# Summing eight experts' weighted outputs: from products and a separate tree of sums to multiply-adds in place

## The reference, cut to what matters

```python
E, D, H = 8, 64, 256                      # experts, channels, hidden
h = gelu(einsum('end,edh->enh', xe, W1) + b1[:, None, :])
y = einsum('enh,ehd->end', h, W2) + b2[:, None, :]      # [expert, token, channel]
sel = take_along_axis(transpose(y, (1, 0, 2)), top_idx[:, :, None], axis=1)
out = (weights[:, :, None] * sel).sum(axis=1)           # two best experts of each token
x = t + out                                             # t: the residual, x2 in the kernel
```

## Time and profile before

| What | Value |
|---|---|
| Runs | 319.32, 317.60, 319.03 us, median 319.03 |
| The profiled execution, its own time | 318.64 us |
| Its span, first to last instruction | 316.9 us |
| TensorE busy | 279.8 us (88%) |
| ScalarE busy | 256.5 us (81%) |
| VectorE busy | 242.5 us (77%) |
| GpSimd busy | 119.8 us (38%) |
| Mean granted TensorE clock | 0.981 of full speed |

### The profile page before, as it was taken

The page is one execution under the profiler, slowest core; times in us unless marked ns, Lnnn a source line. Parts: engine busy times, 40 slices in busy tenths (PEclk is TensorE's granted clock), DMA queues, the critical chain, the costliest instruction groups (busy, mean ns, idle before and its releaser), DMA issues.

```text
span 316.9 us, 8774 instructions
## 1 busy us (share of the span) xinstructions
PE 279.8 (88%) x3434; PEld 191.4 (60%) x3434; DVE 242.5 (77%) x720; ACT 256.5 (81%) x490; POOL 119.8 (38%) x124
## 2 busy tenths in 40 slices
PE   7976998868799898799899999799879999988894
PEld 2552566645467575476577665576667787766462
DVE  6999769799958999659588997586956453589474
ACT  2587678899897999997988899988949898877562
POOL 5040042405142604054466240090836644279130
PEclk9999799989999999999999999999979999999998
DMA  7910000000000000000000000000000000000000
GB/s 157 289 34 0 2 3 4 2 0 0 2 2 4 3 2 2 0 2 8 3 11 2 2 2 0 3 3 8 2 10 2 1 2 2 10 1 11 2 0 17
DMA packets 7190, 4.86 MB, mean 15 GB/s; under 512 B 5089, under 2 KB 6830, under 8 KB 7086
## 3 DMA queue, kind: packets, MB, share of 16 engines
q1 hardware_dynamic: 7150, 4.31, 5.4%
HBM read 2.04 MB, written 0.52 MB: 8 GB/s over the span
## 4 chain that ended last, share of the span: by engine, by line
PE 38%; DVE 27%; ACT 15%; POOL 11%; issue 8%; DMA 1%; SPq 0%; DVEq 0%; ACTq 0%; POOLq 0%
DVE prod L833 4%; PE m_ps L1583 4%; ACT wk L1256 4%; PE zl_ps L1472 4%; PE zh_ps L1469 3%; ACT wk L1251 3%; PE ga_ps L1503 3%; PE ga_ps L1505 3%; PE ga_ps L1504 3%; POOL lx L531 3%; POOL prod L522 3%; PE m_ps L1564 2%; PE m_ps L1566 2%; DVE samp L848 2%; PE m_ps L1447 1%
## 5 line engine op out<-in xcount | busy, mean ns | idle before, releaser
L833 DVE TENSOR_TENSOR prod<-ga_ps,wx 128x480 f32<-128x480 f32 x96 | 61.8, 650 | 36.0 <-PE ga_ps L1505 35.8
L522 POOL TENSOR_TENSOR prod<-prod 128x960 f32<-128x960 f32 (+1 forms) x20 | 39.4, 1969 | 128.2 <-DVE prod L833 128.2
L1503 PE MATMUL ga_ps<-v_all,wk 128*128 128x80 f16 x576 | 80.5, 204 | 6.2 <-DVE prod L833 5.8
L1251 ACT ACTIVATE wk<-zh_ps 128x512 f16<-128x512 f32 x108 | 65.2, 603 | 20.6 <-PE zh_ps L1469 19.5
L1505 PE MATMUL ga_ps<-v_all,wk 128*128 128x80 f16 x576 | 80.5, 204 | 0.0
L1504 PE MATMUL ga_ps<-v_all,wk 128*128 128x80 f16 x576 | 80.5, 204 | 0.0
L1503 PEld LDWEIGHTS ga_ps<-v_all,wk 128*128 128x128 f16 x576 | 57.5, 100 | 18.4 <-issue 9.5
L1256 ACT ACTIVATE wk<-zl_ps 128x512 f16<-128x512 f32 x108 | 65.0, 602 | 0.0
L1504 PEld LDWEIGHTS ga_ps<-v_all,wk 128*128 128x128 f16 x576 | 57.9, 101 | 6.9 <-issue 0.6
L1505 PEld LDWEIGHTS ga_ps<-v_all,wk 128*128 128x128 f16 x576 | 58.1, 101 | 0.0
L1469 PE MATMUL zh_ps<-tab,sel_hi 128*128 128x512 f16 x108 | 42.4, 393 | 6.8 <-ACT wk L1251 5.5
(11 more groups left out here) (278 smaller groups left out, 592.4 us busy)
## 6 DMA issues: line engine op xcount, KB each, us to landing
v_all<-still SPq DMA_DIRECT2D x1, 1440.0 KB, 9.8
h_all<-in_W SPq DMA_DIRECT2D x1, 512.0 KB
w_s<-in_W SPq DMA_DIRECT2D x1, 512.0 KB
x_tok<-in_x SPq DMA_DIRECT2D x1, 384.0 KB, 4.1
out_dram<-x_tok SPq DMA_DIRECT2D x6, 64.0 KB, 1.6
w_high<-w_high SPq DMA_DIRECT2D x1, 256.0 KB, 2.9
const<-in_table SPq DMA_DIRECT2D x1, 218.0 KB, 2.5
vec<-in_vectors SPq DMA_DIRECT2D x1, 132.5 KB
```

What stands on the lines that cost most here:

```text
L522: then(pool.tensor_tensor(p[:, 0:3, :], p[:, 0:3, :], p[:, 3:6, :], ALU.add))
L833: dve.tensor_tensor(prod[q % 2][:].rearrange("p k n -> p (k n)")[:, f * PB * NV:(f + 1) * PB * NV] .rearrange("p (n c l) -> p n c l", n=PB ...
L1251: act.activation(wk[n % WR][:, 0, :], zh_ps[:], ACT.Relu, scale=W_SCALE).then_inc(s_wkh, 1)
L1503: pe.matmul(to, w_h, high, start=True, stop=False)
```

## The change

Each of the six calls of `outputs_in` now issues 16 instructions in place of two: for each expert e and each of the two tiles, `out_s = m_ps * wexp[e] + (x2 or out_s)`, on 64 columns. The weight is a pointer scalar (one number per partition). The two tiles take turns, and each instruction waits through `s_chain` for the one of its own tile before it. `combine` and its places in the tables are gone, and so are `yb`'s use there and `s_y_rd`. VectorE posts `s_out` at the end of the string, and `expert_out` waits for that in place of `s_y_rd`.

```diff
-            def combine(d, i):
-
-                pool.wait_ge(s_y_rd, 2 * d + i + 1)
-                then(pool.tensor_tensor(yb[:, :, 0:4, :], yb[:, :, 0:4, :], yb[:, :, 4:8, :], ALU.add))
-                then(pool.tensor_tensor(yb[:, :, 0:2, :], yb[:, :, 0:2, :], yb[:, :, 2:4, :], ALU.add))
-                then(pool.tensor_tensor(yb[:, :, 0, :], yb[:, :, 0, :], yb[:, :, 1, :], ALU.add))
-                pool.tensor_tensor(out_s[:, d * TP + 2 * i:d * TP + 2 * i + 2, :], yb[:, :, 0, :], x2[:, 2 * i:2 * i + 2, :],
-                                   ALU.add).then_inc(s_out, 1)
...
-                    for i in range(2):
-                        if has_d and n == at["combine"][i]:
-                            combine(j - 1, i)
...
             def outputs_in(d, i):
 
                 dve.wait_ge(s_yt, 2 * d + i + 1)
-                dve.wait_ge(s_chain, seen["wexp"])
-                if i == 1 or d > 0:
-                    dve.wait_ge(s_out, 2 * d + i)
-                for t in range(2):
-                    ins = dve.tensor_tensor(yb[:, t, :, :], m_ps[2 + t].rearrange("p (e c) -> p e c", c=C),
-                                            wexp[:, 2 * i + t, :].unsqueeze(2).to_broadcast([P, E, C]), ALU.mult)
-                ins.then_inc(s_y_rd, 1)
+                acc = [seen["wexp"]] * 2
+                for e in range(E):
+                    for t in range(2):
+                        at = out_s[:, d * TP + 2 * i + t, :]
+                        dve.wait_ge(s_chain, acc[t])
+                        ins = dve.scalar_tensor_tensor(at, m_ps[2 + t][:, e * C:(e + 1) * C], wexp[:, 2 * i + t, e:e + 1],
+                                                       x2[:, 2 * i + t, :] if e == 0 else at, ALU.mult, ALU.add)
+                        if e < E - 1:
+                            acc[t] = mark(ins)
+                ins.then_inc(s_out, 1)
...
                     if d == LAST:
-                        pe.wait_ge(s_y_rd, 2 * d)
+                        pe.wait_ge(s_out, 2 * d)
                 if 2 * m == E and d < CHUNKS - 1:
-                    pe.wait_ge(s_y_rd, 2 * d + 1)
+                    pe.wait_ge(s_out, 2 * d + 1)
```

More of the change, by code:

```diff
@@ L67 @@
              "second_norm": 0}
-POOL_FIRST = {"tap_tree": [4, 14, 23, 31], "combine": [35.5, 22.5], "conv_rstd": 10, "inner_rstd": 21.5, "input_rstd": 27}
+POOL_FIRST = {"tap_tree": [4, 14, 23, 31], "conv_rstd": 10, "inner_rstd": 21.5, "input_rstd": 27}
 PE_MIDDLE = {"input_t": 0, "convolve": [4, 6.5, 6.5, 7.5], "project": 5, "image_t": [9.5, 12], "conv_t": 13.5,
@@ L81 @@
               "bias_rows": 4.5, "router_parts": 12.5, "w1_low": [8, 9.5, 11, 17], "outputs_in": [23.5, 35]}
-POOL_MIDDLE = {"tap_tree": [16.5, 22.5, 25.5, 34.5], "combine": [27, 35.5], "conv_rstd": 21, "inner_rstd": 14,
+POOL_MIDDLE = {"tap_tree": [16.5, 22.5, 25.5, 34.5], "conv_rstd": 21, "inner_rstd": 14,
                "input_rstd": 34}
@@ L99 @@
             "half_expert_weights": 68.5, "lane_sums": [20, 20.5, 29.5, 46.5, 48, 57, 65]}
-POOL_LAST = {"tap_tree": [4, 19.5, 21.5, 35, 42.5, 53.5, 66.5, 71.5], "combine": [37, 53.5], "conv_rstd": 30.5,
+POOL_LAST = {"tap_tree": [4, 19.5, 21.5, 35, 42.5, 53.5, 66.5, 71.5], "conv_rstd": 30.5,
              "inner_rstd": 2.5, "input_rstd": 47, "half_inner_rstd": 44.5, "router_exp": 17.5, "half_router_exp": 71}
@@ L446, in build @@
         s_ysb = sem("s_ysb")
+        s_out = sem("s_out")
         s_yt = sem("s_yt")
-        s_y_rd = sem("s_y_rd")
-        s_out = sem("s_out")
         s_st_out = sem("s_st_out")
```

## The result

The changed kernel's four runs are 326.06, 326.74, 327.61 and 329.09 us, median 327.18, against 319.0 for the kernel before (four runs, 317.6 to 319.32). The ratio estimated from all the runs is 1.0279, with a 95% interval of 1.0244 to 1.0314: slower by 2.8%. The two medians are 8.2 us apart, which is 2.6%. The forecast was 326.4 in a range of 322 to 332. The profiled execution took 326.06 us, its span 324.3, 7.4 more than before.

A forecast was written before the change was run, and what follows sets the result against it. No engine was taken to have much room, TensorE's in-order queue being nearly full, so stops there are lost almost whole. Six call terms (+7.6 us) on 318.64 us, plus half the 0.4 us median offset, gave 326.4 us, range 322 to 332.

The forecast's parts named there:

- The pace: VectorE's 16 multiply-adds start about 0.20 us apart, so each call holds the queue 3.15 us, 1.95 more than before.
- Rival A: Serial string on VectorE: pace 0.32 us, hold 5.1 us per call, together +19.3, 338 us; chance 0.06.
- rival D: Heavy pointer scalar and PSUM read on VectorE: pace 0.27 us, 6.7 us more, 333 us; chance 0.13.
- The 4.5 us computed for a string without overlap: If VectorE's pipe empties before each next start, a call takes 16 x 0.28 us, sum 15.7 us.
- GpSimd: GpSimd some 18 to 20 us less busy without `combine`; VectorE's three copies near 0.96 us at chunks 0 and 1, pair 0.
- The moved wait: TensorE's `expert_out` waits for all 16 instructions (3.27 us) instead of two products (1.3 us), stalling at three calls.
- The terms: Net losses at the six calls, in order: 0.5, 1.55, 0.85, 1.95, 0.8, 1.95 us, sum +7.6 us.
- (1,1): Call at chunk 1, tile pair 1, on the chain, TensorE already standing 1.3 us: all of it, +1.95 us.
- (2,1): Call at chunk 2, tile pair 1, on the chain, TensorE standing 1.20 us for `weigh`: all of it, +1.95 us.
- Rival B: Absorption: TensorE's waits for ScalarE's `wk` (2.6 us) vanish too, +5.0 us, 323.8 us; chance 0.13.
- Rival C: String no dearer than two products: -1.05 + 3e - 0.35 us, e extra per call; 317.8 us without e; chance 0.04.

The follow-up runs named there:

- one_tile_first: Changed kernel with each call running all eight experts of one tile, then of the other; median 344.65 us, ratio 1.0804.
- scrap_sums: Changed kernel with GpSimd still making the four sums of `combine`, on a scrap tile nothing reads; median 329.14 us, ratio 1.0327.
- vector_tree: Kernel before with the four sums of `combine` moved to VectorE, banks set free behind the two products; median 325.31 us, ratio 1.0216.
- late_release: Kernel before with TensorE's `expert_out` held back until VectorE's cast of the weights, at pair 0 of chunks 0 and 1; median 322.70 us, ratio 1.0107.
- fill_wait: Changed kernel with ten idle multiplications on TensorE in its wait behind the call at (1,1); median 325.35 us, ratio 1.0227.
- defer_call: Changed kernel with the call of (1,1) issued in the next body, behind `weigh` and `lane_sum`; median 324.32 us, ratio 1.0193.
- half_string: Changed kernel with eight multiply-adds per call, experts 4 to 7 left out; median 318.71 us, ratio 0.9994.

## Why the prediction was right, point by point

- **The pace.** 0.197 taken, 0.192 measured, in every call; the hold 3.07 us for 3.15. Rival A's 0.32 belongs to a string in which each waits for the one before (`one_tile_first`: 0.32 inside a tile, 0.304 over the call), rival D's 0.27 doesn't occur: neither the pointer scalar nor the PSUM operand costs anything beyond the row L631. The 4.5 us computed for a string without overlap did not come either.
- **GpSimd.** 18.3 us less busy, in the 18 to 20 expected; the copies at 0.96 us as written. The relief is worth 0.9 to 1.6 us in the profile (`scrap_sums`).
- **The moved wait.** Expected stalls 1.2, 1.2, 0.8; found 1.13, 1.13, 0.74. Setting the banks free early removed them (`vector_tree`), and what they cost is the stall less the waits given back (`late_release`).
- **The terms.** Expected 0.5, 1.55, 0.85, 1.95, 0.8, 1.95, sum 7.6; found 0.3, 1.5, 0.7, 3.0, 0.8, 1.4, sum 7.7. The sum owes its closeness to errors of opposite sign (+1.05 at (1,1), -0.2, -0.05, -0.15 and -0.55 elsewhere), and that part is luck.
- **The mis-sized term is (1,1)**: "All of it, +1.95" is right for the call (1.8 in `fill_wait`), but the clock is missing from it, 1.2 us. TensorE had been standing 1.3 us there before, and its clock had fallen then too, from 233.2 to 236.6 us, but behind the projections and for nothing. With 1.9 more its wait is 3.16 us, and the clock was at half from the projections until 242 us. I had costed a stall as its own length only.
- **(2,1)** is smaller than 1.95 by 0.5. TensorE's wait grew by 2.69 - 1.20 = 1.49 us. Before, the call started 0.46 us behind VectorE's `y_s` (0.30 of that idle), and now 0.08 behind. Before and after:

```profile
279.97 0.16 DVE L919 TENSOR_TENSOR y_s<-y_s,y_r 128x2 f32<-128x2 f32 x1
280.43 1.29 DVE L979 TENSOR_TENSOR yb<-m_ps,wexp 128x512 f32<-128x512 f32 x2 [0.30 <-DVE y_s L919]
...
285.32 0.16 DVE L906 TENSOR_TENSOR y_s<-y_s,y_r 128x2 f32<-128x2 f32 x1
285.40 0.48 DVE L967 SCALAR_TENSOR_TENSOR x_tok<-m_ps,wexp,x 128x64 f32<-128x64 f32 x2
```

 The call holds the queue 1.88 us longer (3.07 - 1.19) and starts 0.38 sooner, which makes the 1.5. What the call stood waiting for in the kernel before isn't shown; I had not looked at what stood ahead of it. TensorE's clock fell behind the wait of 2.69 us as well (0.50 from 290 to 292 us), but `defer_call`, without a fall there, takes the same 1.4 us for the step.
- **Rival B** (absorption) did not come: TensorE's waits for `wk` at L1459 are 5.6 us over the span, 5.5 before. ScalarE stood still with TensorE, as written against it.
- **Rival C** needed a short string. `half_string` is that case, and it came out at no change, within 0.3 us of the formula, though by the other path that is told there: that nearness is luck too.

## What to carry to other kernels

Cost an instruction on an engine with time to spare by its place, not by the engine's share: the same 3.1 us string cost 3.0 us more than before ahead of the sum that TensorE stood waiting for and 0.6 us behind it. When a stall of TensorE is lengthened, look at how long it stands there already, and add what the lower clock costs on the work behind it. Before moving work between engines, try moving it within its own queue and away from what it slows: that gave 1.0% here where the exchange lost 2.8%. The string of multiply-adds at the better places wasn't run.

## What the runs showed of the hardware that I had not expected

- A stall has a second price, and its size is set by what comes next. The granted clock went to 0.50 behind TensorE's waits of 3.16 us (cost 1.2 us), 2.69 us (nothing to be seen) and 2.18 us (about 1.5), behind one of 1.4 us in three executions (1.4 to 1.6 us each), behind the kernel before's 1.30 us (nothing to be seen), and in `defer_call` behind waits of 0.60 and 0.45 us. Behind those of 1.13 and 0.98 us it stayed at full in the changed kernel's profile. The same 2.18 us wait left the clock at full once and halved it once, in one execution of `late_release`. So the length of the wait alone doesn't say whether the clock falls.
- GpSimd's sums slow VectorE selectively. Beside them a cast of 128x288 took up to 1.36 us in place of 0.30, `zn` from SBUF 2.33 in place of 0.98, and the multiply-add L779 with both tensors in SBUF up to 1.19 in place of 0.45, while the multiply-adds with one operand in PSUM held 275 to 277 ns as a mean over all 96, those beside `tap_tree` too. The Trainium skill ("GPSIMD Engine Reference", "1. Specifications") says that VectorE contends with GpSimd in its two-port modes and with two inputs from SBUF; that L779 is slowed and a multiply-add with one SBUF input is spared agrees. Which mode the cast and `zn` ran in the traces don't show.
